# A Flamingo-style block on one core: the first stage's queues reordered, two sets of exponentials kept in PSUM, the ninth lag by one maximum

## The reference, cut to what matters

```python
x = x + tanh(g_xattn[0]) * autocorrelation(layernorm(x), ctx, ctx)      # first stage
x = x + tanh(g_ffn[0])   * routed_lora(layernorm(x), W_base, b_base, W_gate, A, B)  # first stage
x = x + tanh(g_xattn[1]) * cross_attention(layernorm(x), ctx, mask, Wq, Wk, Wv, Wo, q_norm_w, k_norm_w)
x = x + tanh(g_ffn[1])   * lora(layernorm(x), lora_A, lora_B, W, bias, lora_weights)

# autocorrelation: over the batch axis of 8 heads, here per channel group and lag
corr = ifft(fft(q) * conj(fft(k))).real
w, idx = top_k(corr, 9); w = softmax(w)
out = sum_i w_i * v shifted by idx_i (clamped at the last row)
# routed_lora: softmax over 8 experts, the two largest kept and renormalised
```

## Time and profile before

| | |
|---|---|
| median of 3 runs | 816.29 us (815.9 to 818.12) |
| the profiled execution's own time | 813.65 us |
| its span | 811.9 us |
| PE busy | 774.1 us (95%), 4224 matmuls |
| PE's weight loads | 631.9 us (78%) |
| DVE busy | 577.2 us (71%), 1283 |
| ACT busy | 412.1 us (51%), 1142 |
| POOL busy | 364.9 us (45%), 420 |
| chain that ended last | PE 68%, DVE 17%, POOL 7%, issue 6% |

### The profile page before, as it was taken

How to read it: one execution, slowest core, us unless ns; L and a number is a source line. 1 busy time by engine, 2 the same in 40 slices (tenths; PEclk the granted TensorE clock), 3 DMA queues, 4 the chain that set the end, 5 groups by cost and what they waited for, 6 DMA issues and landing times.

```text
span 811.9 us, 13195 instructions
## 1 busy us (share of the span) xinstructions
PE 774.1 (95%) x4224; PEld 631.9 (78%) x4224; DVE 577.2 (71%) x1283; ACT 412.1 (51%) x1142; POOL 364.9 (45%) x420
## 2 busy tenths in 40 slices
PE   4699999988999999999999999999999999999998
PEld 1355554667888888888888888888888888888776
DVE  3689999756767777676777766677776666677774
ACT  3246664456545555554565546445555545454521
POOL 1356776646334533643353246424533643254532
PEclk9899999999999999999999999999999999999999
DMA  7300003103100300120031003000310101000002
GB/s 284 115 27 27 26 27 98 45 1 103 29 1 1 105 27 2 42 76 14 1 92 27 14 1 105 27 2 1 104 28 1 52 28 53 1 14 1 1 28 77
DMA packets 16979, 34.61 MB, mean 43 GB/s; under 512 B 2320, under 2 KB 2448, under 8 KB 16656
## 3 DMA queue, kind: packets, MB, share of 16 engines
q1 hardware_dynamic: 16912, 33.78, 13.1%
HBM read 31.67 MB, written 2.10 MB: 42 GB/s over the span
## 4 chain that ended last, share of the span: by engine, by line
PE 68%; DVE 17%; POOL 7%; issue 6%; ACT 1%; DMA 1%; SPq 0%; POOLq 0%; DVEq 0%; ACTq 0%
PE pair L825 17%; PE pair L826 17%; PE pair L827 17%; PE pair L924 4%; PE pair L937 3%; PE pair L986 3%; POOL qkr L512 2%; POOL probn L504 2%; PE pair L926 1%; DVE prod L1160 1%; DVE wlag L1186 1%; POOL wo_lo L498 1%; DVE xres L1243 1%; DVE score L1260 1%; DVE rest L1170 1%
## 5 line engine op out<-in xcount | busy, mean ns | idle before, releaser
L504 POOL TENSOR_TENSOR probn<-prob,erec 128x512 f32<-128x512 f32 x64 | 66.9, 1046 | 162.2 <-DVE erec L1275 162.2
L1299 DVE TENSOR_TENSOR qkn<-pair,qkr 128x640 f32<-128x640 f32 x64 | 52.8, 825 | 91.0 <-POOL qkr L512 91.0
L1280 DVE TENSOR_REDUCE qkss<-qksq 128x5 f32<-128x640 f32 x64 | 52.6, 822 | 86.4 <-ACT qksq L698 86.4
L691 ACT ACTIVATE prob<-score,nmax 128x128 f32<-128x128 f32 x256 | 99.6, 393 | 20.4 <-DVE nmax L1262 18.7
L680 ACT ACTIVATE oT_hi<-pair 128x512 fp32r<-128x512 f32 x64 | 38.2, 597 | 136.2 <-PE pair L827 136.2
L825 PE MATMUL pair<-wq_hi,nT_hi 128*128 128x512 f32 x256 | 105.8, 413 | 0.0
L825 PE MATMUL pair<-wo_hi,oT_hi 128*128 128x512 f32 x256 | 100.8, 394 | 2.8 <-issue 2.8
L827 PE MATMUL pair<-wq_hi,nT_lo 128*128 128x512 f32 x256 | 100.4, 392 | 0.0
L826 PE MATMUL pair<-wo_lo,oT_hi 128*128 128x512 f32 x256 | 100.2, 392 | 0.0
L826 PE MATMUL pair<-wq_lo,nT_hi 128*128 128x512 f32 x256 | 100.2, 391 | 0.0
L827 PE MATMUL pair<-wo_hi,oT_lo 128*128 128x512 f32 x256 | 99.6, 389 | 0.0
(11 more groups left out here) (174 smaller groups left out, 1995.9 us busy)
## 6 DMA issues: line engine op xcount, KB each, us to landing
wq_raw<-in_wq SPq DMA_DIRECT2D x32, 256.0 KB, 2.8
wo_raw<-in_wo SPq DMA_DIRECT2D x32, 256.0 KB, 2.9
wkv_raw<-in_wkv SPq DMA_DIRECT2D x8, 512.0 KB, 4.8
ctxn<-in_ctx_n SPq DMA_DIRECT2D x8, 256.0 KB, 2.9
ctxt<-in_ctx_t SPq DMA_DIRECT2D x8, 256.0 KB, 2.6
out<-wkv_raw SPq DMA_DIRECT2D x8, 256.0 KB, 2.0
xres<-in_x SPq DMA_DIRECT2D x1, 1280.0 KB, 11.7
wbase<-in_wbase SPq DMA_DIRECT2D x1, 1024.0 KB, 9.0
```

Of the source, the lines that this page charges most:

```text
L504: pool.tensor_tensor(probn[:], prob[:], erec[:].unsqueeze(2).broadcast_to([P, HG, P]), ALU.mult).then_inc(normed, 1)
L691: t = act.activation(prob[:, h, :], score[:, h, :], ACT.Exp, bias=nmax[:, h:h + 1], accum_out=esum[:, h:h + 1])
L1280: dve.tensor_reduce(qkss[:], qksq[:], AX.X, ALU.add).then_inc(qk_ss, 1)
L1299: dve.tensor_tensor(qkn[:], qk_bank, qkr[:].unsqueeze(2).broadcast_to([P, HG + 1, P]), ALU.mult).then_inc(qk_nat, 1)
```

## The change

1. **Ninth lag.** `next8` (four maxima) and the copy of its first column into `ninth` become one `tensor_reduce` maximum over `rest8`.
2. **Exponentials stay in PSUM.** The lags' exponentials overwrite `corr_bank` in place (no `elag`); the router's go to a free stretch of `route_bank`. `q_transform(b+1)` and `turn_qk(0)` wait for `picked` (the masked product) in place of `e_lag`.
3. **Router.** The two small copies `nlg` and `two` move from DVE to ACT, ahead of the exponential (`ROUTE` falls from 8 to 6).
4. **Order.** Within a slot, `corr_product(b+1)` goes on DVE ahead of `add_routed`; the context transform on PE and its copies on ACT are those of batch b+2, and `correlation(b+1)` is issued ahead of the second and third part of that transform and of `turn_out`. On ACT, the normalised query rows move to the head of a slot, one batch later. On POOL, `add_bias` and `f_scale` move back.
5. **Start.** `dft` is loaded in two parts, the first ahead of the context; the gates are loaded later and ACT's tanh moves behind the first copies.
6. **Weights.** `wkv_hi`, `wkv_lo`, `wq_hi`, `wq_lo` of the first group are made one slot earlier; `low_wkv` becomes two halves. The tail is reordered.

```diff
-                        act.activation(elag[:, j, :], corr_bank[:, j * P:(j + 1) * P], ACT.Exp,
+                        act.activation(corr_bank[:, j * P:(j + 1) * P], corr_bank[:, j * P:(j + 1) * P], ACT.Exp,
                                        bias=ntop[:, j:j + 1]).then_inc(e_lag, 1)
...
                 def q_transform(b):
                     pe.wait_ge(f_norm, b + 1)
-                    need(pe, e_lag, CH * b)
+                    need(pe, picked, PICK * b - 1)
...
-                    for j in range(CH):
-                        t = dve.max(next8[:, j, :], rest8[:, j, :])
-                    t.then_inc(lag9, 1)
-                    dve.wait_ge(lag9, 3 * b + 1)
-                    dve.tensor_copy(ninth[:, :, 0], next8[:, :, 0]).then_inc(lag9, 1)
+                    dve.tensor_reduce(ninth[:, :, 0], rest8[:], AX.X, ALU.max).then_inc(lag9, 1)
...
                 def route_exponents(b):
-                    act.wait_ge(h_step, ROUTE * b + 3)
-                    act.activation(eg[:], lg[:, 0:E], ACT.Exp, bias=nlg[:]).then_inc(h_exp, 1)
+                    act.wait_ge(h_step, ROUTE * b + 2)
+                    act.activation(two[:, 0:2], lg8[:, 0:2], ACT.Copy).then_inc(h_exp, 1)
+                    act.activation(nlg[:], lg8[:, 0:1], ACT.Copy, scale=-1.0).then_inc(h_exp, 1)
+                    act.wait_ge(h_exp, 3 * b + 2)
+                    act.activation(eg, lg[:, 0:E], ACT.Exp, bias=nlg[:]).then_inc(h_exp, 1)
...
                 def a_slot(b):
-                    if has(b - 2):
-                        add_bias(b - 2)
                     low_turned_ctx(b)
                     if has(b - 3):
                         low_rows(b - 3)
-                    if b == 4:
+                    if b == 3:
                         low_wkv(0)
-                    if b in (5, 6):
-                        for c in (2 * b - 10, 2 * b - 9):
+                    if b in (4, 5):
+                        for c in (2 * b - 8, 2 * b - 7):
                             low_wq(0, c)
                     lag_weights(b)
+                    if has(b - 2):
+                        add_bias(b - 2)
...
                     pick_lags(b)
                     if has(b - 1):
                         add_lagged(b - 1)
+                    corr_product(b + 1, 0)
+                    corr_product(b + 1, 1)
                     if has(b - 2):
                         add_routed(b - 2)
-                    if has(b + 2):
+                    if b < 2:
                         f_statistics(b + 2)
                     out_products(b)
-                    corr_product(b + 1, 0)
-                    corr_product(b + 1, 1)
+                    if b >= 2 and has(b + 2):
+                        f_first(b + 2)
                     if has(b - 1):
-                        route(b - 1)
+                        route_first(b - 1)
+                    if b >= 2 and has(b + 2):
+                        f_last(b + 2)
+                    if has(b - 1):
+                        route_last(b - 1)
```

More of the change, by code:

```diff
@@ L95, in flamingo_kernel @@
             kfb = early("kfb", [P, 4, D])
-            rest8, rest9, elag, wlag = (early(n, [P, CH, P]) for n in ("rest8", "rest9", "elag", "wlag"))
+            rest8, rest9, spare, wlag = (early(n, [P, CH, P]) for n in ("rest8", "rest9", "spare", "wlag"))
             op = [early(f"op{i}", [P, D]) for i in range(4)]
@@ L212, in flamingo_kernel @@
         ld_ct = sem("a_ctx_turned_loaded")
-        ld_dft = sem("a_dft_loaded")
+        ld_dft = [sem(f"a_dft_loaded{i}") for i in range(2)]
         ld_w = [sem(f"a_weights_loaded{i}") for i in range(4)]
@@ L370, in _ @@
                 load_batches(0)
+                sp.dma_start(dft[:, 0:V_IM + 1, :], dft_d[:, 0:V_IM + 1, :]).then_inc(ld_dft[0], 16)
                 load_ctx(0)
-                sp.dma_start(dft[:], dft_d[:]).then_inc(ld_dft, 16)
-                sp.dma_start(gates_in[:], gates[:]).then_inc(ld_g, 16)
+                sp.dma_start(dft[:, V_IM + 1:N_DFT, :], dft_d[:, V_IM + 1:N_DFT, :]).then_inc(ld_dft[1], 16)
                 load_batches(1)
                 load_ctx(1)
+                sp.dma_start(gates_in[:], gates[:]).then_inc(ld_g, 16)
                 load_turned_ctx(0)
@@ L477, in sums, with low_wkv @@
                     pool.tensor_tensor(op[2][:], op[2][:], op[3][:], ALU.subtract).then_inc(o_sum, 1)
-                def low_wkv(g):
+                def low_wkv(g, halves=(0, 1)):
                     pool.wait_ge(wkv_h, g + 1)
-                    pool.tensor_tensor(wkv_lo[g % 2][:], wkv_raw[:], wkv_hi[g % 2][:].bitcast(F32),
-                                       ALU.subtract).then_inc(wkv_l, 1)
+                    for i in halves:
+                        w = slice(i * D, (i + 1) * D)
+                        pool.tensor_tensor(wkv_lo[g % 2][:, w], wkv_raw[:, w], wkv_hi[g % 2][:, w].bitcast(F32),
+                                           ALU.subtract).then_inc(wkv_l, 1)
                 def low_wq(g, c):
@@ L529, in a_slot @@
                         g_scale(b - 2)
+                    sums(b)
                     if has(b + 2):
                         f_scale(b + 2)
-                    sums(b)
                 def slot(n):
@@ L774, in slot @@
                         high_batch(turning(n))
-                act.wait_ge(ld_g, 16)
-                act.activation(gate[:], gates_in[:], ACT.Tanh).then_inc(tanhed, 1)
                 normalise(nx[:], 0, f_sc, f_root, f_norm)
@@ L857, in inverse, with base_products @@
                     pe.matmul(wr_bank, dft[:, O_INV2, :], op[2][:], start=False, stop=True).then_inc(f_out, 1)
-                def base_products(b):
+                def base_products(b, chunks=range(CH)):
                     need(pe, h_added, b)
-                    for c in range(CH):
+                    for c in chunks:
                         pe.matmul(base_bank, n1T[:, c, :], wbase[:, c, :], start=(c == 0), stop=False)
@@ L1098, in slot @@
                         feed_forward(batch(n, FEED))
-                pe.wait_ge(ld_dft, 16)
+                pe.wait_ge(ld_dft[0], 16)
+                ctx_transform(0, 0)
                 q_transform(0)
-                for i in range(3):
-                    ctx_transform(0, i)
+                ctx_transform(0, 1)
+                pe.wait_ge(ld_dft[1], 16)
                 correlation(0)
+                ctx_transform(0, 2)
+                ctx_transform(1, 0)
                 for b in range(B - 1):
@@ L1153, in f_statistics @@
                         dve.wait_ge(ld_x[2], 16)
-                    statistics(b, f_stat, f_mv, f_stats, f_root)
+                    f_first(b)
+                    f_last(b)
                 def corr_product(b, i):
```

141 lines of the change are left out of this document (85 added, 56 removed).

## The result

The changed kernel takes 819.99 us (median of 18 runs, 815.17 to 824.25), the kernel before beside it 816.32 (18 runs, 813.87 to 818.12): a ratio of 1.0047, 95% interval 1.0031 to 1.0063. It is slower by 3.7 us; the prediction said 813.1, faster, with a range that ended just short of rival A's 819.9. The profiled execution took 821.45, with a span of 819.7 and a mean granted clock of 0.983 (before: 813.65, 811.9, 0.994).

A forecast was written before the change was run, and what follows sets the result against it. It took a DVE-paced first stage, then a PE-bound rest, with a new loop through ACT setting the slot. Gains 2.2 + 3.2 + 1.0 - 4.3 + 1.1 = 3.2 off median 816.29 gave 813.1; range just short of 805.9 to just short of 819.9.

The forecast's parts named there:

- rival A: PE's clock falls at new gaps in slots 1, 3, 4 and 5, costing 4 × 1.7 = 6.8: 819.9; chance 0.2.
- slots 1 and 2: First stage, same ACT list with first items missing: together 32.3 against 33.3, gain 1.0.
- slots 3 to 6: First stage: 3 × 18.8 + 16.5 = 72.9 against 68.6, loss 4.3.
- The start, slot 0, the tail: Pick 0 at 14.75, gain 2.2; slot 0 13.55, gain 3.2; pick 7 to scores 29.7, gain 1.1.
- The loop through ACT: From r, when DVE has the router's maximum, ACT's list delays the masked product to r + 7.4; slot 16.4.
- POOL late in slots 3 to 5: POOL's low halves hold the lag weights 2.4 us; slots 18.8 each, PE idle some 2.8.
- The clock: PE's clock behind 2.8 us gaps: evidence between double price and full clock; a fall taken in slot 0 only.
- The second stage as a block: PE-bound rest, matmuls unchanged: moves as a block with the first scores' start.
- The sum and the median: Gain of 3.2 makes the profiled 813.65 into 810.4; taken off the median 816.29, 2.6 above, it gives 813.1.
- Rival D: On DVE the masked product still waits for POOL; no price of its own, since DVE waits there for ACT anyway.
- B: POOL isn't late, port relief pays: slots 3 to 5 take 16.4, 7.2 more gain, 805.9; chance 0.2.
- C: The loop is half a microsecond longer per slot, seven times: 3.5 gone, 816.6; chance 0.2.

The follow-up runs named there:

- e10: Changed kernel plus unused filler matmuls on PE ahead of slot 1's query transform, the turned lags in slots 3 to 5 and two second-stage gaps: 812.07 us.
- e3: Kernel before with only the changes inside DVE's steps, no reordering and no split load: 807.86 us, ratio 0.9884.
- e6: Kernel before with the changes inside DVE's steps and the changed kernel's start, no other reordering: 805.46 us.
- e1: Changed kernel with POOL's low halves of the second stage's weights moved behind its lag weights, bias and scales in slots 3 to 5: 809.27 us, ratio 0.9908.
- e13: e1 with POOL's low halves one place later, behind the scales of the second residual's normalisation: 806.95 us.
- e4: Changed kernel with the lags' exponentials in SBUF again and the query's transform waiting for them, not the masked product: 823.92 us, ratio 1.0092.
- e7: Changed kernel's order on all engines and split load, with the old steps of the kernel before inside: 823.87 us, ratio 1.0102.
- e12: e1 with ACT's lag exponentials first, POOL's turned-context low half later, and SP loading context rows ahead of the turned context: 809.44 us.
- e14: e12 with POOL's low halves one place later, the same move as in e13: 803.88 us.
- e8: e1 plus unused filler matmuls ahead of slot 1's query transform and in two gaps of the second stage's start: 807.75 us.
- e11: e6 plus unused filler matmuls ahead of the query's transform in slots 0 and 1 and in two second-stage gaps: 801.95 us, ratio 0.9818.
- e15: e14 plus unused filler matmuls in slot 0 ahead of the context's last product and in two second-stage gaps: 799.38 us, ratio 0.9805.

## Why the prediction was wrong

By its own steps, in the changed kernel, with the prediction's number first:

| step | predicted | changed kernel | with its clock held (e10) |
| --- | --- | --- | --- |
| pick 0 at | 14.75 | 14.95 | 15.53 |
| slot 0 | 13.55 | 13.7 | 13.5 |
| slots 1 and 2 | 32.3 | 35.1 | 32.6 |
| slots 3 to 6 | 72.9 | 77.2 | 73.5 |
| pick 7 to the scores | 29.7 | 30.2 | 30.2 |
| scores to those of slot 3 | 29.6, as before | 32.8 | 29.7 |

- **The start, slot 0, the tail**: right to 0.5 us. That the start is worth about 2 us was shown by itself (2.4 by the medians, 2.1 by the first scores).
- **The loop through ACT** (masked product at r + 7.4, slot 16.4): right. It was 7.6 here (82.6 to 90.18), and with POOL out of the way the slot was 16.45.
- **POOL late in slots 3 to 5, 18.8 each, PE idle near 2.8**: right in place and size (18.93 at full clock, idle 2.60), shown by the move that takes it away.
- **The clock**, the step that failed. The prediction put the gaps of 2.8 us "between" a fall and none, took none, so that its sum holds nothing for falls in slots 1, 3, 4 and 5, and gave rival A 0.2. A's condition came true in each of its four slots. Its price was 6.8 for the four; compared with the fillers they cost 2.5, 1.3, 1.2 and 1.2, or 6.2. The sum names no idle time of PE in slot 1; it was 2.59 us, ahead of the query's transform, for DVE's masked product.
- **The second stage as a block**, which "whatever the first stage gains or loses moves": wrong by 3.2 us in the profiled executions. Their first gaps met a full clock before and a falling one now. But the order alone doesn't decide this. The gaps of 1.93 and 2.10 us are the same in every kernel without fillers there, and the stretch took 29.6, 31.2 or 32.8 us in the profiled executions as the clock fell behind none, one or both: the old order with the new steps had one fall (e3, e6), and kernels in the new order, further changed, none (e1, e13), one (e4, e7, e12) or two (e14). Beside the experiments, only 11 of 50 runs of the kernel before had the mean clock of its profiled one, 0.994 (813.6 to 815.8 us); the others had 0.987 to 0.991 (815.9 to 818.9). These have no trace, so where their clock fell isn't shown; the second stage's start is the likely place.
- **The sum and the median.** The prediction took its gain off the median and so carried over 2.6 us between the profiled execution and the median, without a reason. If these are falls of the kernel before, the 813.1 already held them. Compared like with like, the sum gave 810.4 for an execution with no fall in the second stage, and the profiled one with the clock held took 812.63: 2.2 short, by the last column pick 0 0.8, slots 1 and 2 0.3, slots 3 to 6 0.6, the tail 0.5. That 812.07 is only 1.0 under the forecast is partly luck, and so is A's 819.9 beside the measured 819.99: A has its four falls right, and the 2.6 stands in for the rest. The profiled execution, 821.45, is 11.05 above the 810.4, and the table's misses add up to it: 0.2 + 0.15 + 2.8 + 4.3 + 0.5 + 3.2 = 11.15.
- **Rival D** (masked product still stalls: "no price of its own, as DVE waits there for ACT anyway"): wrong in its reasoning, though it didn't occur. The wait and the stall come one after the other; undoing the relief cost 3.9 us. The prediction had read one stalled product of about 1 us in the kernel before; in the new order three of the four stalled with the relief undone.
- **B** (POOL not late) was wrong, but what it described is what the experiments made: 809.3 with one move, and 806.95 with slots of 16.5, beside its 805.9, with the second.
- **C** (a loop longer by half a microsecond) was wrong: the slot was 16.45 for 16.4.

So the change consists of a part worth 8.5 us (the steps; 9.0 beside the runs of its own round), one worth 2.4 (the start), and an order that cost 14.5 beyond them: 805.46 to 819.99. These hold in this sequence only: the steps are worth 8.5 in the old order and 3.9 in the new one (823.87 to 819.99). With fillers in both the step is from 801.95 to 812.07, 10.1 for the order itself, of which the prediction's 3 × 2.4 = 7.2 is POOL's lateness in slots 3 to 5. The other 4.4 is clock: 7.9 for the falls of the new order, less 3.5 for those of the old.

## What to carry to other kernels

When a reordering opens a gap on TensorE in a loop that PE nearly fills, price the gap with what runs behind it at half the clock, and do it also for gaps in later stages that are there already: they cost in some executions and not in others, so one profile isn't their price. Before a forecast is taken off a median, ask what sets the profiled execution apart from it. Before a step is moved on one engine, list what stands behind it in that engine's list and in every queue that waits for it, loads included; here three moves each made a new thing late (`wlagn`, then `g_sc`, then a load). And test a change in halves: this one held 11 us of gain and 14.5 of loss.

## What the hardware showed that I had not expected

- The length of a gap alone doesn't decide whether the clock falls. Slot 0's gap ahead of the same product, in the changed kernel and in the first experiment's, whose lists are the same there:

```profile
20.03 1.95 PE L850 MATMUL pair<-ctxn,dft 128*128 128x512 f32 x2 [2.83 <-ACT kfa L619]
```

```profile
20.07 1.12 PE L850 MATMUL pair<-ctxn,dft 128*128 128x512 f32 x2 [2.85 <-ACT kfa L619]
```

  The granted clock of 20 to 24 us is 0.57 in the first and 1.00 in the second. It also differs within one execution. In the kernel with ACT's exponentials first, two gaps of 2.58 us stand ahead of the same instructions in slots 3 and 4; behind the first the router took 1.91 (above), behind the second:

```profile
99.12 1.12 PE L851 MATMUL pair<-ctxn,dft 128*128 128x512 f32 x2 [2.58 <-DMA ctxn<-in_ctx_n]
100.08 1.09 PE L909 MATMUL pair<-wag,n1T 128*128 128x136 f32 x8
```

  The slots took 19.9 and 18.2 us. In the changed kernel's profiled execution gaps of 1.93 and 2.10 us cost the clock, and the same two in that of the kernel before did not. The Trainium skill (TensorE: Matmul & The Clock Gate, section "Why this matters for your kernels") warns against idle gaps between bursts of matmuls; the trace agrees, and shows it for gaps that I had taken as safe, though not at every one.
- The changed kernel's 18 runs spread over 9 us, and time and mean clock go together: 815.17 at 0.992, 819.81 at 0.985, 824.25 at 0.979. In four kernels with fillers in both stages (e8, e10, e11, e15), at 0.997 to 1.000 in all runs but one (0.993), the spread was 1.3 to 3.5 us over four runs each.
- Four exponentials written into the PSUM bank that they read took 1.11 us, beside 1.14 from PSUM to SBUF. ScalarE: Activation LUTs in the Trainium skill, cited in the prediction, has writing PSUM as quicker; it is, by 0.03 us for the four, in every slot.
